# Two running maxima instead of three, halved ahead of the last unit, with code factors built from exponents, in a quantised decoder layer

## The reference

```python
def _pot_scale(x):                      # a power of two
    m = jnp.maximum(jnp.max(jnp.abs(x)), 1e-08)
    return jnp.exp2(jnp.ceil(jnp.log2(m / 127.0)))

def fq_floor(x):
    s = _pot_scale(x)
    return jnp.clip(jnp.floor(x / s), -128.0, 127.0) * s
...
h = layernorm(x) * fq_round(gamma) + fq_round(beta)
qkv = fq_floor(fq_floor(h) @ fq_round(w_qkv))           # 16 heads of 64
dots = fq_floor(einsum('bhnd,bhmd->bhnm', q, k) * temp)
attn = fq_floor(softmax(dots))
out = fq_floor(fq_floor(attn @ v) @ fq_round(w_out))
x = layernorm(x + out)
...                                                    # linear cross attention, then an int8 MLP
```

## Time and profile before

| what | value |
|---|---|
| median of 3 runs | 468.15 us |
| the profiled execution | 468.85 us |
| its span, first to last instruction | 467.1 us |
| VectorE (DVE) busy | 406.2 us, 87% |
| ScalarE (ACT) busy | 346.7 us, 74% |
| TensorE (PE) busy | 238.0 us, 51% |
| GpSimd (POOL) busy | 145.5 us, 31% |
| granted TensorE clock, mean | 0.699 of full speed |
| HBM read and written | 7.75 MB and 1.58 MB |

### The profile page before, as it was taken

How to read it: one execution, slowest core, us unless ns; L and a number is a source line. 1 busy time by engine, 2 the same in 40 slices (tenths; PEclk the granted TensorE clock), 3 DMA queues, 4 the chain that set the end, 5 groups by cost and what they waited for, 6 DMA issues and landing times.

```text
span 467.1 us, 6743 instructions
## 1 busy us (share of the span) xinstructions
PE 238.0 (51%) x1534; PEld 101.2 (22%) x1541; DVE 406.2 (87%) x1293; ACT 346.7 (74%) x789; POOL 145.5 (31%) x321
## 2 busy tenths in 40 slices
PE   1588864878577733333333333049995818115031
PEld 0553311323221210000000000013342716011031
DVE  3969997989699999999999999867977986977967
ACT  3679884979899955999999999926776655428133
POOL 2400000001000001999999999960000006420010
PEclk9999997999655555555555555559999766557557
DMA  7600000000344521699899998790003000000002
GB/s 265 158 1 1 0 1 1 22 22 25 135 180 180 200 94 67 146 202 201 200 201 200 203 202 180 135 224 3 1 1 125 29 0 1 1 0 0 0 0 92
DMA packets 84215, 43.21 MB, mean 92 GB/s; under 512 B 69063, under 2 KB 74455, under 8 KB 84058
## 3 DMA queue, kind: packets, MB, share of 16 engines
q1 hardware_dynamic: 82618, 42.69, 35.8%
q10 hardware_dynamic: 1568, 0.21, 0.3%
HBM read 7.75 MB, written 1.58 MB: 20 GB/s over the span
## 4 chain that ended last, share of the span: by engine, by line
DVE 34%; ACT 27%; PE 19%; issue 16%; ACTq 2%; DMA 1%; DVEq 0%
ACT mem L948 20%; PE ps L471 17%; DVE mem L1070 5%; DVE mem L1228 5%; DVE d_max L1073 3%; DVE mem L1491 2%; ACT mem L882 2%; DVE m L1628 2%; DVE m L1629 2%; ACT mem L918 2%; DMA gbc<-in_L_attn_ln_beta 1%; ACTq L948 1%; DVE c L1069 1%; DVE mem L1279 1%; DVE mem L1498 1%
## 5 line engine op out<-in xcount | busy, mean ns | idle before, releaser
L471 PE MATMUL ps<-mem 64*128 64x256 bf16 (+5 forms) x1182 | 180.5, 353 | 117.7 <-DVE row_max L1320 80.1
L948 ACT ACTIVATE mem<-mem,neg_max 128x256 f32<-128x256 int16 x256 | 125.8, 492 | 9.2 <-DVE neg_max L1069 9.2
L471 PEld LDWEIGHTS ps<-mem 64*128 64x128 bf16 (+3 forms) x1188 | 65.9, 119 | 224.6 <-DVE row_max L1320 108.7
L1320 DVE CUSTOM_DVE_ANT_0 mem<-ps,fold,c 128x256 int16<-128x256 f32 x256 | 110.9, 471 | 0.2 <-DVE fold L1070 0.2
L429 POOL TENSOR_SCALAR mem<-mem,r_now 128x256 int16<-128x256 f32 x176 | 81.6, 485 | 76.5 <-DVE r_now L1069 76.3
L1228 DVE TENSOR_TENSOR mem<-mem 128x1024 bf16<-128x1024 bf16 x76 | 49.6, 686 | 5.6 <-ACT mem L882 2.9
L898 ACT ACTIVATE mem<-ps,c 128x1024 bf16<-128x1024 f32 x48 | 48.4, 1295 | 1.5 <-PE ps L471 1.5
L948 ACT ACTIVATION_READ_ACCUMULATOR mem<-mem,neg_max x256 | 47.5, 185 | 0.0
L918 ACT ACTIVATE mem<-ps,c 128x1024 int16<-128x1024 f32 x32 | 36.4, 1211 | 12.7 <-DVEq L1263 7.4
L1073 DVE TENSOR_REDUCE d_max<-ps 128x1 f32<-128x1024 f32 (+1 forms) x34 | 37.9, 1125 | 3.0 <-PE ps L471 3.0
L429 POOL TENSOR_SCALAR bv_fine<-mem,r_now 128x256 int16<-128x256 f32 x80 | 36.8, 482 | 2.3 <-DVE r_now L1069 2.2
(11 more groups left out here) (203 smaller groups left out, 362.5 us busy)
## 6 DMA issues: line engine op xcount, KB each, us to landing
mem<-mem SPq DMA_DIRECT2D x64, 256.0 KB, 2.3
mem<-in_L_attn_w_qkv SPq DMA_DIRECT2D x1, 1536.0 KB, 9.6
mem<-in_x SPq DMA_DIRECT2D x2, 512.0 KB, 5.4
mem<-in_x SPq DMA_DIRECT2D x1, 1024.0 KB, 5.5
out<-mem SPq DMA_DIRECT2D x4, 256.0 KB, 2.2
xattn_matrix<-mem SPq DMA_DIRECT2D x1, 512.0 KB
mem<-in_L_attn_w_out SPq DMA_DIRECT2D x1, 512.0 KB, 4.8
mem<-in_L_ffn_W SPq DMA_DIRECT2D x2, 256.0 KB, 5.1
```

The costliest lines, as they stand in the source:

```text
L471: return te.matmul(o_, l_, r_, start=start, stop=stop)
L948: ins = sc.activation(e_ring[:, u % 4, pos], y_ring[:, u % 4, pos], ACT.Exp, scale=scale_reg, bias=neg_max[:, u % 4, pos:pos + 1], accum_o ...
L1320: ins = ve.tensor_tensor_reduce(y_ring[:, slot, pos], ps[:, 2 * slot + pos // 2, (pos % 2) * N:(pos % 2 + 1) * N], shift, col("g_dots"), - ...
```

## The change

The three running maxima become two. Units 0 and 1 of ScalarE go straight into them; unit 2 becomes a fold. At the end of a pass VectorE merges the two, reduces the column of its own maxima, folds the upper half of the running maximum onto the lower (512 columns), and writes the diagonal of its own column already then. Behind the last unit it folds that unit's halves together, folds them into the running maximum (512 columns), reduces 512 columns, and takes the diagonal with the larger of the two values in one instruction (`scalar_tensor_tensor`: identity times column, larger of that and the diagonal that stands there).

Code factors (`g_qkv`, `g_fine`, `g_o`, `g_proj`) come straight from `scale_of`: the constant from which the exponent bits are subtracted carries the other scale (`numerator`), so the product behind it goes. The factor of `shift` is worked out in `temperature()`, at the start of the qkv code pass, up to the scale of dots. For o, the two reductions of 512 columns in PSUM become one of 1024, and an identity times `GROW` is written during the products with v, at group 21.

```diff
-        run_max = at(168, [3, UNIT], BF16)
+        run_max = at(168, [2, UNIT], BF16)
+        ident_g = diag[:, 1]
...
-                        sc.activation(run_max[:, nth] if nth < 3 else abs_t[:, nth % 3],
+                        sc.activation(run_max[:, nth] if nth < 2 else abs_t[:, nth % 3],
...
-                    act.wait_ge(sem("o_last"), 2)
+                    act.wait_ge(sem("o_last"), 1)
...
-            def across_bf(bank):
-                ts(diag_b[:, 0], ident_b[:], col("m"), None, ALU.mult).then_inc(sem("diagonals"), 1)
+            def across_bf(bank, value, spread):
+                ve.scalar_tensor_tensor(diag_b[:, 0], spread, value, diag_b[:, 0], ALU.mult, ALU.max)\
+                    .then_inc(sem("diagonals"), 1)
                 across_take(1, bank, col("x"))
...
-                ins = ts(inv_out.bitcast(I32), bits, -1.0, float(0x7F000000), ALU.mult, ALU.add)
+                ins = ts(inv_out.bitcast(I32), bits, -1.0, over, ALU.mult, ALU.add)
...
+            def numerator(name):
+                ts(col("n_" + name), col(name).bitcast(I32), float(0x3F800000), None, ALU.add)
+                return ts(col("k_" + name), col(name), HALF_RANGE, None, ALU.mult)
...
                 ts(col("temp_grow"), col("temp"), GROW, None, ALU.mult).then_inc(sem("dots_grow"), 1)
+                link(ts(col("s_qt"), col("s_qq"), col("temp"), None, ALU.mult))
+                link(ts(col("f_qt"), col("s_qt"), 1.0e-30, None, ALU.max))
+                link(ve.reciprocal(col("f_qt"), col("f_qt")))
+                link(ts(col("f_qt"), col("f_qt"), FLOOR, None, ALU.mult))
...
-                        if 3 <= nth < total - 1:
+                        if 2 <= nth < total - 1:
+                            run = run_max[:, nth % 2]
                             dve.wait_ge(sem(f"{phase}_max_act"), len(acts) + nth + 1)
-                            dve.wait_ge(sem(f"{phase}_folded"), nth + 1)
-                            ve.tensor_tensor(run_max[:, k], run_max[:, k], abs_t[:, k], ALU.max)\
+                            dve.wait_ge(sem(f"{phase}_folded"), nth + 2)
+                            ve.tensor_tensor(run, run, abs_t[:, nth % 3], ALU.max)\
                                 .then_inc(sem(f"{phase}_folded"), 1)
...
-                for j in others:
-                    link(ve.tensor_tensor(run_max[:, k], run_max[:, k], run_max[:, j], ALU.max))
+                link(ve.tensor_tensor(run, run, run_max[:, 1], ALU.max))
                 dve.wait_ge(sem(f"{phase}_max_dve"), (iters + 1) * len(dves))
                 link(ve.tensor_reduce(col("md"), d_max[:, 0:iters * len(dves)], AX.X, ALU.max))
-                link(ts(cb[:, 0:1], col("md"), grow, None, ALU.mult))
+                link(ve.tensor_tensor(run[:, 0:half], run[:, 0:half], run[:, half:], ALU.max))
+                link(ts(diag_b[:, 0], ident_b[:], col("md"), grow, ALU.mult, ALU.mult))
                 dve.wait_ge(sem(f"{phase}_max_act"), len(acts) + total)
-                link(ve.tensor_tensor(run_max[:, k], run_max[:, k], abs_t[:, k], ALU.max))
-                link(ve.tensor_reduce(col("m"), run_max[:, k], AX.X, ALU.max))
-                link(ts(col("m"), cb[:, 0:1], col("m"), None, ALU.max))
+                link(ve.tensor_tensor(last[:, 0:half], last[:, 0:half], last[:, half:], ALU.max))
+                link(ve.tensor_tensor(run[:, 0:half], run[:, 0:half], last[:, 0:half], ALU.max))
+                link(ve.tensor_reduce(col("m"), run[:, 0:half], AX.X, ALU.max))
...
-            across_bf(7)
-            scale_of(col("x"), 1, col("s_qkv"), col("i_qkv"), factor=col("k_hw"))
-            ts(col("g_qkv"), col("s_hw"), col("i_qkv"), None, ALU.mult).then_inc(sem("qkv_scale"), 1)
+            across_bf(7, col("m"), ident_b[:])
+            scale_of(col("x"), 1, col("s_qkv"), col("g_qkv"), factor=col("k_s_hw"), over=col("n_s_hw"), done="qkv_scale")
...
-            dve.wait_ge(sem("qkv_scale"), 1)
...
-            link(ts(col("g_dots"), col("s_qq"), col("temp"), col("i_dots"), ALU.mult, ALU.mult))
+            link(ts(col("g_dots"), col("i_dots"), col("s_qt"), None, ALU.mult))
             ts(col("ns_dots"), col("s_dots"), -1.0, None, ALU.mult).then_inc(sem("dots_scale"), 1)
-            dve.wait_ge(sem("dots_scale"), 1)
-            link(ts(col("shift"), col("g_dots"), 1.0e-30, None, ALU.max))
-            link(ve.reciprocal(col("shift"), col("shift")))
             for k in range(2):
-                ins = ts(shift[:, k * P:(k + 1) * P], ones[:], col("shift"), FLOOR, ALU.mult, ALU.mult)
+                ins = ts(shift[:, k * P:(k + 1) * P], ones[:], col("f_qt"), col("s_dots"), ALU.mult, ALU.mult)
...
-            scale_of(col("x"), 1, col("s_attn"), col("i_attn"))
-            ts(col("g_fine"), col("i_attn"), 1.0 / FINE, None, ALU.mult).then_inc(sem("attn_scale"), 1)
+            scale_of(col("x"), 1, col("s_attn"), col("g_fine"), over=float(0x7F000000 - (14 << 23)), done="attn_scale")
             link(ts(col("s_av"), col("s_attn"), col("s_qkv"), None, ALU.mult))
-            ts(col("k_av"), col("s_av"), HALF_RANGE, None, ALU.mult)
-            dve.wait_ge(sem("attn_scale"), 1)
+            numerator("s_av")
...
+                if grp == 21:
+                    link(ts(ident_g, ident[:], GROW, None, ALU.mult))
...
             link(ve.tensor_reduce(col("m"), run_o[:, 0], AX.X, ALU.max))
+            link(ts(diag_b[:, 0], ident_b[:], col("m"), None, ALU.mult))
...
-            for k in range(2):
-                dve.wait_ge(sem("av_group"), B * GROUPS - 1 + k)
-                absmax(d_max[:, k:k + 1], ps[:, last_bank + k, :]).then_inc(sem("o_last"), 1)
-            dve.wait_ge(sem("o_last"), 2)
-            link(ts(cb[:, 0:1], d_max[:, 0:1], d_max[:, 1:2], GROW, ALU.max, ALU.mult))
-            link(ts(col("m"), cb[:, 0:1], col("m"), None, ALU.max))
-            across_bf(6)
-            scale_of(col("x"), 1, col("s_o"), col("i_o"), factor=col("k_av"))
-            ts(col("g_o"), col("s_av"), col("i_o"), None, ALU.mult).then_inc(sem("o_scale"), 1)
+            dve.wait_ge(sem("av_group"), B * GROUPS)
+            absmax(d_max[:, 0:1], ps[:, last_bank:last_bank + 2].rearrange("p a n -> p (a n)"))\
+                .then_inc(sem("o_last"), 1)
+            dve.wait_ge(sem("o_last"), 1)
+            across_bf(6, d_max[:, 0:1], ident_g)
+            scale_of(col("x"), 1, col("s_o"), col("g_o"), factor=col("k_s_av"), over=col("n_s_av"), done="o_scale")
             link(ts(col("s_ow"), col("s_o"), s4[:, 3:4], None, ALU.mult))
-            ts(col("k_ow"), col("s_ow"), HALF_RANGE, None, ALU.mult)
-            dve.wait_ge(sem("o_scale"), 1)
+            link(numerator("s_ow"))
...
-            scale_of(col("x"), 1, col("s_proj"), col("i_proj"), factor=col("k_ow"))
-            ts(col("g_proj"), col("s_ow"), col("i_proj"), None, ALU.mult).then_inc(sem("proj_scale"), 1)
-            dve.wait_ge(sem("proj_scale"), 1)
+            scale_of(col("x"), 1, col("s_proj"), col("g_proj"), factor=col("k_s_ow"), over=col("n_s_ow"), done="proj_scale")
```

More of the change, by code:

```diff
@@ L897, in batch @@
                         s = 2 * (u % ring)
-                        sc.activation(run_max[:, k] if first and k < 3 else abs_t[:, k % 3],
+                        sc.activation(run_max[:, k] if first and k < 2 else abs_t[:, k % 3],
                                       ps[:, s:s + 2].rearrange("p a n -> p (a n)"),
@@ L1100, in across_take, with scale_of @@
                 link(ins)
-            def scale_of(grown, n, s_out, inv_out, factor=HALF_RANGE, done=None):
+            def scale_of(grown, n, s_out, inv_out, factor=HALF_RANGE, over=float(0x7F000000), done=None):
                 bits = s_out.bitcast(I32)
@@ L1185, in _ @@
             link(ts(col("s_hw"), s4[:, 3:4], s4[:, 2:3], None, ALU.mult))
-            ts(col("k_hw"), col("s_hw"), HALF_RANGE, None, ALU.mult)
+            numerator("s_hw")
             w_piece(2)
@@ L1205, in max_pass @@
                 dve.sem_inc(sem(f"{phase}_max_dve"), len(dves))
-                dve.sem_inc(sem(f"{phase}_folded"), 6)
+                dve.sem_inc(sem(f"{phase}_folded"), 5)
                 prime = 2 * STAGES if phase == "dots" else 0
@@ L1223, in max_pass @@
                         nth = i * len(acts) + acts.index(u)
-                        k = nth % 3
-                        if 3 <= nth < total - 1:
+                        if 2 <= nth < total - 1:
+                            run = run_max[:, nth % 2]
                             dve.wait_ge(sem(f"{phase}_max_act"), len(acts) + nth + 1)
-                            dve.wait_ge(sem(f"{phase}_folded"), nth + 1)
-                            ve.tensor_tensor(run_max[:, k], run_max[:, k], abs_t[:, k], ALU.max)\
+                            dve.wait_ge(sem(f"{phase}_folded"), nth + 2)
+                            ve.tensor_tensor(run, run, abs_t[:, nth % 3], ALU.max)\
@@ L1229, in max_pass @@
                                 .then_inc(sem(f"{phase}_folded"), 1)
-                k = (total - 1) % 3
```

(6 more changed lines are left out.)

## The result

| | before | after |
|---|---|---|
| median of 20 runs each, same chips | 469.19 us (468.12 to 470.39) | 467.76 us (466.75 to 468.98) |
| profiled execution | 468.85 us, span 467.1 | 467.07 us, span 465.4 |

The ratio is 0.9971, with a 95% interval of 0.9961 to 0.9981: 1.36 us faster (0.9 to 1.8). The direction is as forecast. The time is not: 467.76 lies above 466.0 and above the range's end of 467.1.

A forecast was written before the change was run, and what follows sets the result against it. VectorE, late at the passes' ends, was taken to bound the kernel, so only its instructions' sum counts. Terms 0.82 + 1.10 - 0.03 + 0.09 + 0.18 = 2.16 us off 468.15 gave 466.0; 8-in-10 range 464.9 to 467.1.

The forecast's parts named there:

- Inside the passes: Maximum passes: the extra fold per pass falls in VectorE's idle time and costs nothing; without that cover 0.63 us a pass.
- a fold waits for a fold: Rival, maximum passes: each fold must await the one just before it, 4.2 us slower, 472.4 us; chance 0.05.
- Half folds at the rate of float32: Rival, ends of the maximum passes: folds of 512 take 0.70 us each, time 467.7 us; chance 0.05.
- the longer entry: Rival, start of qkv code pass: VectorE's added steps make TensorE wait, up to 0.78 us lost, 466.8 us; chance 0.07.
- Dots: End of the dots pass and its scale: 0.70 us saved in the tail and 0.40 behind the scale, 1.10 together.
- qkv: End of the qkv maximum pass and its scale: 0.75 us saved in the tail and 0.07 behind it, 0.82 together.
- the tail that both share: VectorE's linked steps at the end of each maximum pass: 0.75 us saved for qkv, 0.70 for dots.
- o: Around the scale of o: one reduction for two and changed diagonals; VectorE, which sets this stage, gains 0.09 us.
- proj: Scale of the projection: ScalarE waits for `g_proj` at once, so 0.23 less 0.05 saves 0.18 us.
- attn: Scale of attn: `g_fine` goes and `numerator` adds an unlinked instruction, 0.03 us lost.
- the anchor: Starting time of the forecast: 468.15 us, the median of the runs shown; 2.16 us off it gives 466.0.
- The clock: Rival, products with v and qkv code pass: TensorE's clock rise does not come forward with the work, 467.0 us; chance 0.15.

The follow-up runs named there:

- experiment 4: After without the halves (one fold of 1024 and one reduction of 1024 at each pass's end): 467.13 us against 468.77 for before, ratio 0.9962.
- experiment 1: Before with only the new end of the two maximum passes and its diagonal: 467.60 us against 469.18 for before, ratio 0.9967.
- experiment 7: After with four more one-column products on VectorE ahead of the qkv maximum pass, read by nothing: 467.01 us in one run.
- experiment 6: Unread TensorE products added until right before the products with v: after so changed 464.48 us (0.9895), before so changed 466.41 us (0.9943).
- experiment 3: 28 and 8 unread TensorE products added ahead of the products with v: after so changed 467.01 us (0.9956), before so changed 469.38 us (0.9994).
- experiment 8: Unread TensorE products added at five places: after without halves 460.69 us (0.9798), before so changed 462.38 us (0.9851).

## Why the prediction was right and wrong

**What bounds the kernel at these places** was right: VectorE is late at a pass's end, and ScalarE's idle time shrank by what the string lost. That "the new order [...] brings nothing by its order" is shown by experiment 4, which is no slower at the median and 0.12 us shorter a pass. The prediction stopped short of its consequence: if the order brings nothing, the halving loses.

**Inside the passes**, right: the extra fold was taken from idle time, the passes kept their 35.95 and 47.3 us, and the rival in which a fold waits for a fold did not happen (experiment 1). *Half folds at the rate of float32* is refuted by 0.43, *the longer entry* by the idle 0.58 that was left.

**The terms.** Dots 1.11 for 1.10, qkv 0.72 for 0.82; the tail that both share gave 0.67 and 0.65 instead of 0.75 and 0.70 (experiment 1). From start to start the three half folds took 1.39 where 1.32 was taken, the reduction 0.72 for 0.70, the early diagonal 0.29 for 0.27: small errors of the links, all one way. o gave 0.07 for 0.09 and proj 0.09 for 0.18; profiles of after and its variants lie 0.3 apart in this row, so little can be made of that. attn is the one mis-sized in kind: 0.29 lost where 0.03 was taken, of which 0.27 is the time between two instructions that the change did not touch (experiment 7). The sum is 1.70 instead of 2.16. By the prediction's own sign ("a time above 467.2 makes the sum wrong") it was wrong, by 0.46. The runs don't place it closer: 1.36 (0.9 to 1.8), again 2.1 (1.4 to 2.9), and 1.93 in experiment 6.

**The step that failed** is the anchor, "the same 2.16 off 468.15 gives 466.0". The three runs of before lay within 0.4 us of each other; 20 of them span 2.3 us and have their median at 469.19. That alone is 1.04 of the 1.77 us by which the forecast was low. The other 0.73 is the gain, 2.16 against the medians' 1.43. The profiled execution's own sum, 466.7, was nearer, but I went by the median of three. Neither part alone leads out of the range: from 469.19 the full 2.16 gives 467.0, and 1.43 off 468.15 gives 466.7. Both together do, and the range up to 467.1 had room for one rival but none for the anchor.

The later runs show what the three may have been. The 69 runs of before that were taken beside the experiments fall into two kinds by their mean granted clock: 29 at 0.698 or 0.699, with a median of 468.31 us (467.44 to 469.48), and 40 at 0.692 to 0.697, with a median of 469.90 (468.48 to 471.06). The first profile of before is of the first kind (0.699), the second, with the late rise in the qkv code pass, of the second (0.693). Of the profiles without added products of TensorE, all six with the early rise have 0.698 or 0.699, and both with the late one 0.693 or 0.694. The three, 468.12 to 468.48, lie where the first kind lies (their own clocks aren't known). That all three came out so was luck; the fault was to take their spread of 0.4 us for the kernel's. Of after's 32 runs 25 had 0.698 or more, with a median of 467.16. So the medians compare mixtures, and within this kind the two kernels are 1.15 us apart. Why after is of it more often stays open.

**The clock**, given 0.15 as a rival. Windows around the rise in before, then in after:

```profile
315.00:315.50 0.50, 0.50 (x6) 0.13 (x2) 0.50 (x2) 0.07 (x1) 0.00 (x0) 0.50 1.00 200
315.50:316.00 0.50, 0.50 (x6) 0.14 (x4) 0.50 (x2) 0.50 (x1) 0.00 (x0) 0.97 0.00 0
```

```profile
314.00:314.50 0.50, 0.50 (x5) 0.13 (x2) 0.50 (x3) 0.50 (x2) 0.00 (x0) 0.50 0.00 0
314.50:315.00 0.50, 0.50 (x6) 0.14 (x5) 0.43 (x3) 0.50 (x1) 0.00 (x0) 0.98 0.00 0
```

The products with v began at 310.84 before and at 308.87 after. So the rise came 4.7 us behind them in before and 5.6 in after: it came forward with the work, but by 1.0 us of the 1.97, and the stage is 0.37 longer for it. In this pair the rival happened, at about 0.4 us and not the 1.0 it was given. It is no property of the change, though: in the second profile of before the rise came 5.7 us behind (stage 44.42), and with four small products more 3.3 (43.46). It is the spread between executions, which I took for absent because three runs agreed.

How the stage hangs on this lag can be read from the nine profiles that enter it at 0.50. Their lags run from 3.3 to 6.1 us and their lengths from 43.46 to 44.58, and 42.13 us (the length with the clock at 1.00 throughout, experiments 3, 6 and 8) plus 0.40 us for each us of lag gives every one of them within 0.03, whichever edits the kernel had.

In the qkv code pass the rise came 3.3 us behind the first product with codes in before and 3.5 in after. The Trainium skill, "TensorE: Matmul & The Clock Gate", section "Part 1: The HAM clock gate", says that the beat is free-running and not reset by the kernel; one kernel with lags of 4.7 and 5.7 us agrees with that. The 7.6 us of experiment 8 on before (470.01 less 462.38) show what the cold entries cost here.

## What to carry to other kernels

Where one engine is late at the end of a pass, only the sum of its instructions counts; splitting an operation to do half of it early can pay only if the engine waits there. Before a forecast of a few parts in a thousand, ask how far single executions lie apart: an anchor of three runs was off by half of the forecast effect. Compare two traces stage by stage, and read the rise of the clock in each stage that TensorE enters cold before an edit is credited or blamed. Such entries are also the larger prize: keeping TensorE busy up to them took 7.6 us off before, against the 1.7 of this change, but the products of experiment 3, with 3.0 us of idle time behind them, brought nothing in the profile of after.

## What the hardware showed that was not expected

- TensorE's clock was down again at 308.0, with 28 added products ended at 302.9 and only ten short ones from 305.9 to 307.2 behind them, and one program's runs fell into two groups 2.6 us apart (experiment 3).
- The length of the products with v was 42.13 us plus 0.40 for each us from the first product to the rise of the clock, within 0.03 in nine profiles of seven programs.
- An unchanged pair of small VectorE instructions started 0.08 to 0.12 us apart in before and 0.39 in after, in two profiles of each; the cause wasn't found.
- A fold of 512 bf16 took 0.43 us against 0.69 for 1024: 0.17 of either is fixed, which is why three halves cost more than they save.
